# First attention of a four-stage block: heads paired by parity, 128-wide stationary parts, three context buffers

## The reference

```
def _proj(W, b, x):
    return jnp.einsum('oi,bil->bol', W, x) + b[:, None]
def _L0_xattn_ref(x_query, x_key, x_value, Wq, bq, Wk, bk, Wv, bv, Wo, bo):
    B, D, L = x_query.shape            # D = 64 rows, L = 512, 8 heads
    h = 8; Lh = L // h                 # 64 columns of a head
    q = _proj(Wq, bq, x_query)         # 64 x 64 weights, over the rows
    k = _proj(Wk, bk, x_key)
    v = _proj(Wv, bv, x_value)
    qh = q.reshape(B, D, h, Lh).transpose(2, 0, 1, 3)   # kh, vh likewise
    scores = jnp.einsum('hbdk,hbek->hbde', qh, kh) / sqrt(Lh)
    p = jax.nn.softmax(scores, axis=-1)
    xh = jnp.einsum('hbde,hbek->hbdk', p, vh)
    return _proj(Wo, bo, xh.transpose(1, 2, 0, 3).reshape(B, D, L))

x = x + _L0_xattn_ref(_layernorm(x), ctx, ctx, ...)     # the stage here
x = x + _L0_ffn_ref(_layernorm(x), ...)                 # quantised feed-forward
x = x + _L1_xattn_ref(_layernorm(x), ctx, ctx, ...)     # linear attention
x = x + _L1_ffn_ref(_layernorm(x), ...)                 # dense layer and experts
```

## Time and profile before

| | |
|---|---|
| runs (device us) | 753.6, 755.01, 752.37; median 753.6 |
| the profiled execution | 751.84, of which 750.0 from its first to its last instruction |
| PE, DVE, ACT, POOL busy | 678.8, 607.0, 490.1, 377.2 us |
| matrix records on PE | 6649 in 750.0 us |
| `attention0` | from 223 to 319 us |
| granted TensorE clock | 0.972 on average; 0.84 from 222 to 228 us |

### The profile page before, as it was taken

How to read it: one execution, slowest core, us unless ns; L and a number is a source line. 1 busy time by engine, 2 the same in 40 slices (tenths; PEclk the granted TensorE clock), 3 DMA queues, 4 the chain that set the end, 5 groups by cost and what they waited for, 6 DMA issues and landing times. The chain is left out here.

```text
span 750.0 us, 17745 instructions
## 1 busy us (share of the span) xinstructions
PE 678.8 (91%) x6649; PEld 347.7 (46%) x6649; DVE 607.0 (81%) x973; ACT 490.1 (65%) x885; POOL 377.2 (50%) x328
## 2 busy tenths in 40 slices
PE   4999999999987777599999959999999999986997
PEld 2454554545445555444444414444444444443643
DVE  6878788888754767769999859899999999986555
ACT  3888867676724666566767716788787787874440
POOL 2000009999952666431221316777776786752224
PEclk9999999999999999889999977999999999998999
DMA  6144655566425333013344220000000000014606
GB/s 171 56 139 124 200 196 139 135 164 159 114 44 157 67 82 80 11 34 68 65 80 69 58 38 0 2 2 0 1 2 1 1 2 1 1 29 85 114 1 224
DMA packets 92600, 54.71 MB, mean 73 GB/s; under 512 B 76964, under 2 KB 76964, under 8 KB 92516
## 3 DMA queue, kind: packets, MB, share of 16 engines
q1 hardware_dynamic: 91764, 53.06, 28.1%
q10 hardware_dynamic: 752, 0.52, 0.3%
HBM read 32.00 MB, written 4.19 MB: 48 GB/s over the span
## 5 line engine op out<-in xcount | busy, mean ns | idle before, releaser
L1435 POOL TENSOR_TENSOR query_qn<-query_eq,query_rq 128x1024 f32<-128x1024 f32 x64 | 121.9, 1904 | 53.5 <-DVE query_rq L1369 51.6
L687 ACT ACTIVATE keys_ek<-keys_psK,keys_mk 128x512 f32<-128x512 f32 x128 | 86.8, 683 | 39.6 <-DVE keys_mk L537 37.7
L537 DVE TENSOR_REDUCE keys_mk<-keys_psK 128x2 f32<-128x1024 f32 x64 | 77.9, 1218 | 16.8 <-PE keys_psK L746 16.6
L1360 DVE TENSOR_REDUCE query_mq<-query_psQ 128x16 bf16<-128x1024 f32 x64 | 75.4, 1179 | 5.1 <-PE query_psQ L1523 4.9
L1454 ACT ACTIVATE query_eq<-query_psQ 128x1024 f32<-128x1024 f32 x64 | 65.1, 1017 | 21.4 <-PE query_psQ L1536 21.4
L1366 DVE TENSOR_REDUCE query_lq<-query_eq 128x16 f32<-128x1024 f32 x64 | 77.3, 1207 | 2.2 <-ACT query_eq L1454 2.1
L1545 PE MATMUL query_psX<-all_ident,query_qn 128*128 128x128 f32 x512 | 70.8, 282 | 0.4 <-ACT query_qT L1461 0.4
L757 PE MATMUL keys_psT<-all_ident,keys_ek 128*128 128x128 f32 x512 | 70.8, 282 | 0.0
L769 PE MATMUL keys_psG<-keys_eT,keys_cT 128*64 128x512 f32 x256 | 69.0, 617 | 1.0 <-issue 0.9
L757 PEld LDWEIGHTS keys_psT<-all_ident,keys_ek 128*128 128x128 f32 x512 | 55.5, 142 | 28.3 <-issue 19.9
L1461 ACT ACTIVATE query_qT<-query_psX 128x1024 f32<-128x1024 f32 x64 | 65.4, 1022 | 1.1 <-PE query_psX L1545 1.1
(11 more groups left out here) (273 smaller groups left out, 1440.8 us busy)
## 6 DMA issues: line engine op xcount, KB each, us to landing
all_ring<-in_L_ffn_w_down_dram SPq DMA_DIRECT2D x8, 688.0 KB, 4.4
all_ring<-in_L_ffn_w_gate_dram SPq DMA_DIRECT2D x10, 512.0 KB, 4.8
all_ring<-in_L_ffn_w_up_dram SPq DMA_DIRECT2D x10, 512.0 KB, 3.7
all_x_res<-in_x_dram SPq DMA_DIRECT2D x4, 1024.0 KB, 6.0
att_ctx_n<-in_ctx_dram SPq DMA_DIRECT2D x16, 256.0 KB, 3.2
out_dram<-all_x_res SPq DMA_DIRECT2D x16, 256.0 KB, 2.2
all_cf<-in_ctx_dram SPq DMA_DIRECT2D x15, 256.0 KB, 2.7
att_w_nat<-in_L_ffn_W_dram SPq DMA_DIRECT2D x4, 256.0 KB, 4.3
```

What stands on the lines that cost most here:

```text
L537: dve.tensor_reduce(mk[:, c, :], psK[c % 2][:, :, :], X, ALU.max, negate=True).then_inc(mk_ok, 1)
L687: act.activation(ek[t % 2][b][:, c, :], psK[c % 2][:, b, :], ACT.Exp, bias=mk[:, c, b:b + 1], accum_out=le[t % 2][:, b, c:c + 1]).then_inc ...
L1360: dve.tensor_reduce(mq[g % 2][:, :, 0:HEADS], psQ[g % 2][:, :, :].rearrange("p b (h d) -> p b h d", d=D), X, ALU.max, negate=True).then_in ...
L1435: pool.tensor_tensor(qn[m % 2][:, :, :], eq[m % 3][:, :, :], rq[m % 2][:, :].unsqueeze(2).broadcast_to([P, 2 * HEADS, D]), ALU.mult).then_ ...
```

## The change

Heads are now paired by parity: r is the parity of a head and c its pair, so that heads 2c and 2c+1 stand side by side in the 512 columns. The projections take the 128 columns of a pair as one stationary part of 64 x 128 (8 products for queries and 8 for keys a tile, where there were 16 and 16), and `projected` takes the probabilities of a pair likewise (8 for 16). The layout of `pn` is changed for that, so that POOL writes it through a permuted view. The moving operand of `values` and the place of the result in x are read and written in pieces of 64 columns, and the addition to x is two instructions on DVE, one for each parity, where it was one. The context has three buffers: loads stand two tiles ahead of their use in SP's queue, and a transposing pair now also waits for the pair before it.

```diff
-KEYS_CTX = 16 * (TILES // 2)
+KEYS_CTX = (16 * (TILES // 2), 16 * (TILES // 2), 0)
...
-    sp.dma_start(k.ctx_n[i % 2][:, :], nat[i]).then_inc(k.ctx_in[i % 2], 16)
+    sp.dma_start(k.ctx_n[i % 3][:, :], nat[i]).then_inc(k.ctx_in[i % 3], 16)
...
-        pn = s.sb("pn", [P, 2, NC, D])
+        pn = s.sb("pn", [P, NC, 2, D])
...
                 sp.wait_ge(wlo_ok, o + 1)
+                wait(sp, w_in, 32 * o)
...
-            load_context0(sp, a, k, 0)
-            load_context0(sp, a, k, 1)
+            for i in range(3):
+                load_context0(sp, a, k, i)
             for i in range(TILES):
-                if i >= 2:
-                    sp.wait_ge(v_ps, i - 1)
-                    load_context0(sp, a, k, i)
+                if 1 <= i < TILES - 2:
+                    sp.wait_ge(v_ps, i)
+                    load_context0(sp, a, k, i + 2)
...
-                pool.tensor_tensor(pn[:, :, :, :], ex[:, :, :, :], rs[:, :, :].unsqueeze(3).broadcast_to([P, 2, NC, D]),
+                pool.tensor_tensor(pn[:, :, :, :].rearrange("p c r e -> p r c e"), ex[:, :, :, :], rs[:, :, :].unsqueeze(3).broadcast_to([P, 2, NC, D]),
                                    ALU.mult).then_inc(pn_ok, 1)
...
-                dve.scalar_tensor_tensor(out=k.x[:, t, :].rearrange("p (r n) -> p r n", r=2),
-                                         in0=psWO[:, :, NC * D:2 * NC * D], scalar=k.bo2[:, :],
-                                         in1=k.x[:, t, :].rearrange("p (r n) -> p r n", r=2),
-                                         op0=ALU.add, op1=ALU.add).then_inc(x_ok, 1)
+                for r in range(2):
+                    x = k.x[:, t, :].rearrange("p (c r d) -> p r c d", r=2, d=D)[:, r, :, :]
+                    dve.scalar_tensor_tensor(out=x, in0=psWO[:, r, NC * D:2 * NC * D].rearrange("p (c d) -> p c d", d=D),
+                                             scalar=k.bo2[:, :], in1=x, op0=ALU.add, op1=ALU.add).then_inc(x_ok, 1)
...
-                            for r in range(2):
-                                at, h = (m * NC + c) * D, r * NC + c
-                                mm = pe.matmul(psQK[HALF[r], b, at:at + D], x[HALF[b], h * D:(h + 1) * D],
-                                               k.wT0[HALF[b], m, :], start=False, stop=True, skip_group_check=True)
+                            at = (m * NC + c) * D
+                            mm = pe.matmul(psQK[:, b, at:at + D], x[HALF[b], c * P:(c + 1) * P], k.wT0[HALF[b], m, :],
+                                           start=False, stop=True, skip_group_check=True)
...
-                                       ctx_n[i % 2][HALF[b], r * NC * D:(r + 1) * NC * D],
+                                       ctx_n[i % 3][HALF[b], :].rearrange("p (c r d) -> p r c d", r=2, d=D)[:, r, :, :],
...
-                        for r in range(2):
-                            mm = pe.matmul(psWO[HALF[r], b, c * D:(c + 1) * D], pn[HALF[b], r, c, :],
-                                           k.wT0[HALF[b], 3, :], start=True, stop=True)
+                        mm = pe.matmul(psWO[:, b, c * D:(c + 1) * D], pn[HALF[b], c, :, :].rearrange("p r e -> p (r e)"),
+                                       k.wT0[HALF[b], 3, :], start=True, stop=True)
```

More of the change, by code:

```diff
@@ L861, in attention0 @@
         s = Scope(nc, ctx, "att0")
-        k.ctx_n = [s.sb(f"ctx_n{p}", [P, L]) for p in range(2)]
+        k.ctx_n = [s.sb(f"ctx_n{p}", [P, L]) for p in range(3)]
         late = k.late = Shared()
@@ L961, in stats @@
             def stats(t):
-                dve.wait_ge(x_ok, t + 1)
+                dve.wait_ge(x_ok, 2 * t + 2)
                 wait(dve, mv_ok, t)
@@ L1063, in projections @@
                 pe.wait_ge(xn_ok, i + 1)
-                pe.wait_ge(ctx_in[i % 2], KEYS_CTX + 16 * (i // 2) + 16)
-                for m, x in enumerate((xn[i % 2], ctx_n[i % 2])):
+                pe.wait_ge(ctx_in[i % 3], KEYS_CTX[i % 3] + 16 * (i // 3) + 16)
+                for m, x in enumerate((xn[i % 2], ctx_n[i % 3])):
                     for c in range(NC):
                         for b in range(2):
-                            for r in range(2):
-                                at, h = (m * NC + c) * D, r * NC + c
-                                mm = pe.matmul(psQK[HALF[r], b, at:at + D], x[HALF[b], h * D:(h + 1) * D],
-                                               k.wT0[HALF[b], m, :], start=False, stop=True, skip_group_check=True)
+                            at = (m * NC + c) * D
+                            mm = pe.matmul(psQK[:, b, at:at + D], x[HALF[b], c * P:(c + 1) * P], k.wT0[HALF[b], m, :],
+                                           start=False, stop=True, skip_group_check=True)
                 mm.then_inc(qk_ps, 1)
@@ L1094, in projected @@
                 pe.wait_ge(pn_ok, t + 1)
-                wait(pe, x_ok, t)
+                wait(pe, x_ok, 2 * t)
                 for c in range(NC):
                     for b in range(2):
-                        for r in range(2):
-                            mm = pe.matmul(psWO[HALF[r], b, c * D:(c + 1) * D], pn[HALF[b], r, c, :],
-                                           k.wT0[HALF[b], 3, :], start=True, stop=True)
+                        mm = pe.matmul(psWO[:, b, c * D:(c + 1) * D], pn[HALF[b], c, :, :].rearrange("p r e -> p (r e)"),
+                                       k.wT0[HALF[b], 3, :], start=True, stop=True)
                 mm.then_inc(w_ps, 1)
@@ L1977, in program @@
         k.b_in = s.sem("b_in")
-        k.ctx_in = [s.sem(f"ctx_in{p}") for p in range(2)]
+        k.ctx_in = [s.sem(f"ctx_in{p}") for p in range(3)]
         with ExitStack() as ctx_m:
```

## The result

The changed kernel is slower: 763.04 us median of five executions (755.59 to 765.07), where the kernel before has 753.4 (751.56 to 755.01), a ratio of 1.011 with a 95% interval from 1.008 to 1.015. Run again beside the experiments it has 762.6 against 753.1, ratio 1.015 (1.010 to 1.019). Forecast were 756.8 and a range up to 762: the direction is right, the size is not, and the median lies 1 us beyond the range. The sum had +3.2 us; the medians lie 9.6 us apart.

A forecast was written before the change was run, and what follows sets the result against it. Instruction fetch was taken to bound the first attention before the change. Terms of 0.1 + 1.2 + 1.6 + 0.3 gave +3.2 us, taking the median from 753.6 to 756.8 us, with a range of 747 to 762.

The forecast's parts named there:

- Fetch bounds the kernel before: First attention: instruction fetch, about 127 load and product pairs per 3.98 us, gives 5.33 of each 5.40 us beat.
- Rival B: Slower: the fetch gap is a fixed cost per block, say 0.8 us, not a rate; +10, 766.8 us; chance 0.08.
- Wide loads cost 0.051 us a step more: Loads of 64*128 for queries, keys and `projected`: 0.112 us a step for 0.061, so 0.41 us per eight-step group.
- Rivals A and C: A: wide loads hide, steps near 0.061, 745.3 us, chance 0.13. C: halves load in turn, 0.223, about 800, chance 0.03.
- The new beat 5.31: Time from one tile's scores to the next: 5.31 us, bound by PE and ACT's copy, with no fetch gap left.
- change of shape: Between scores and `projected`, now of different tile shapes: about 0.1 us a change, from 0 to 0.2.
- DVE's addition: Addition to x as two halves: 0.2 us extra on 0.745, hidden but at two places and in the last tile.
- POOL's permuted write: Writing `pn` permuted: no cost up to 0.9 us of room; 0.1 us a beat if twice as long.
- 13 beats 70.3: Tiles 2 to 15: 69.0 us plus 0.7 for POOL's extra work and 0.6 for DVE's quantising; against 70.2, +0.1.
- First two beats 4.27 and 5.47: First two beats of the stage, not fetch-bound, pay the wide loads in full: +0.4 and +0.8, together 1.2 us.
- Before S0 +1.6: Before the stage's first scores: projections at 1.2 GHz take 0.22 us a step until about 229.4; +1.6 us (1.0 to 1.9).
- The end +0.3: Stage's end: last `projected` +0.4, last addition +0.2, and 0.3 back because `projected` can start earlier; +0.3 us.

The follow-up runs named there:

- first profile: Profiled execution of the changed kernel with no further edit, the quickest of its five: 755.59 us, against a median of 763.04.
- kernel kept at work: Changed kernel plus twelve unread products of 512 columns behind the first bias products, in PE's idle time before its first projections: 754.31 us, ratio 1.0031.
- second profile: Identical changed kernel run again, no edit; its profiled execution is listed at 761.5 us, the run's median is 762.64, ratio 1.0146.
- three buffers with the shift: Kernel before with three context buffers, POOL's row scales and DVE's quantising steps moved two tiles later: 749.83 us, ratio 0.9974.

## Why the prediction was right in direction and short in size

- **Fetch bounds the kernel before.** Right. Each gap ends 1.3 to 1.5 us after its instruction packet. Taking 32 pairs from a tile took 7.3 us from 13 beats with the shapes unchanged, and in the changed kernel no gap by "issue" is left between two matrix records from 238 to 320 us. Rival B (gaps fixed per block) falls: the blocks are still crossed, seven times in 35.8 us, without a gap.
- **Wide loads cost 0.051 us a step more.** Right: 0.112 was taken, 0.112 measured. Removing the width from queries and keys gave 0.85 us a beat. Rivals A and C fall with it. The Trainium skill (TensorE: Matmul & The Clock Gate, LDWEIGHTS (loading the stationary operand)) gives 107 ns for a load of 128 columns. The trace agrees, with 112 ns a step, in which two row halves load side by side.
- **The new beat 5.31.** 5.33 measured, in eleven of the 13 beats (to 0.01). A change of shape was put at 0.1: 0.62 to 0.63 for 0.61.
- **DVE's addition.** In the first profile two halves take 0.88 us as a pair, +0.13 where +0.2 was taken; hidden, as said. POOL's permuted write takes 1043 ns for 1042: nothing.
- **13 beats 70.3.** 69.9 measured. POOL's extra work reached `projected` by 0.38 and made one beat 0.45 longer, where 0.7 was put; the first quantising step made one beat 0.18 longer and the second none, where 0.6 was put together. Both were put too high, by 0.7 in all, and the beat 0.02 too low, thirteen times. Near in sum, and fetch's gain is spent on the loads.
- **First two beats 4.27 and 5.47.** In the kernel kept at work they are 4.29 and 5.48. In the first profile, where the clock rose only during the first, they are 4.99 and 5.33. In the usual execution they are 6.84 and 9.30, and 6.33 follows.
- **Before S0 +1.6.** This is the step that failed. From the first product to ACT's copy it took 3.72 us for 2.04, +1.7, so the price of the wide loads is right (S0 moved by only 1.24, since the first product came 0.44 sooner after the bias product). But the term and the two beats behind it assumed that the clock rises at 229.4, as before. It rose at 233.3 in the execution of 755.6 us and only at 249.1 in the usual one: some 24 us at 1.2 GHz in place of 3.4. The stage lasts 106.7 us there and 98.8 when PE is kept at work. The difference of 7.9 us is the missing part; between the medians of these kernels, each against its own kernel before, it is 9.5 - 2.3 = 7.2.
- **The end +0.3.** +0.95 in the first profile. The wider `projected` and the addition added 0.47 and 0.12 (0.4 and 0.2 taken), but the last `projected` began 5.90 after S15, not 5.2: POOL was still preparing weights, and what was put at -0.3 is +0.36:

```profile
317.75 1.20 PE L1098 MATMUL att_psWO<-all_wT,att_pn 64*128 64x64 f32 x16 [2.77 <-POOL att_pn L943]
```

The error was to take the time at which the clock rises as a property of the stage. It depends on what PE does meanwhile, and the change alters that: at 1.2 GHz the wide loads take 0.216 us a step (in the second profile the queries begin at 225.81 and the keys at 227.54, eight steps later), and the clock doesn't rise for a long time. Four kernels show it from both sides: PE kept at work before (754.3), narrow loads at the start (753.5), wide loads at the start alone (758.4), wide queries and keys alone (both outcomes in one kernel). With PE kept at work the changed kernel is 2.3 us over the kernel before, near the +3.2 of the sum, but that is in part luck. Its profile has about 0 before S0 where the sum has +1.6, because no low level is left there at all; and about +1.7 at the end where the sum has +0.3: 0.95 as in the first profile, and 0.8 because the level falls earlier there. The terms between, +1.2 and -0.3 us, fit the sum's 1.2 and 0.1.

What stays open is why the level ends after 6.8 us in some executions: one of eleven of the changed kernel by its time, one of four with wide loads at the start alone by its clock, and three of nine with `projected` narrow. The one that was profiled began its stage 1.2 us later than the other (224.25 against 223.05); whether that decides wasn't tried. Nor is it shown what in PE's work brings the level up; the runs show only which edits do.

A forecast from a sum of rows should have had this as a rival of its own: rows 10 showed a mean clock of 0.84 to 0.88 just where the change makes each step longer.

## What to carry to other kernels

Count PE's load and product pairs in each stage against the rate at which instruction packets come, and merge products only where the wider load doesn't lie on the way to the engine that is waited for; here `projected` could be widened and the projections couldn't. Where an edit makes products slower in a stage that begins at the low clock level, ask whether PE's work there still brings the level up, run it several times, and compare the granted clock of each execution before trusting one profile. Some cheap products in an idle time before such a stage show within one run whether the clock is the cause.

## What the runs showed of the hardware

- In the second profile the level was 1.2 GHz for 24 us, though PE is shown as busy for 5.9 to 6.0 of every 6 us from 229 on, with 70 to 88 records of 64*128 loads and short products in each 6 us. The Trainium skill (TensorE: Matmul & The Clock Gate, What's actually happening) describes a clock gate that is released by PE's activity. From the busy column of this trace the release couldn't have been told.
- In four kernels the clock fell for 3.4 us in the middle of the stage, each time 0.6 to 0.9 us after PE went on from a wait of 1.3 to 1.9 us for POOL (from 278.96 after the product at 278.35 in the kernel with `projected` alone wide). In a fifth, three buffers with the shift, it fell twice, 0.2 and 1.5 us after waits of 1.45 and 1.78 us by "issue". Such a wait doesn't suffice: the kernel with three buffers has one of 2.41 us and no fall. In the kernel with `projected` alone wide the beat that held the fall was 2.9 us longer than its neighbours, more than twice the wait of 1.27.
- An instruction packet of about 127 pairs started 1.1 to 2.0 us after PE had gone on into the block before, took 0.9 to 1.4 us, and let PE go on 1.3 to 1.5 us after its end: 3.98 us a block on average.
- The fetch isn't an exact clock: 154 pairs a tile ran at 4.51 us for some tiles in a row, quicker than 4.83, and came back to 4.73 on average.
